# A recurrent mixer's pieces in a new order, two half-width products side by side, and a feed-forward's second weights prepared a turn later

## The reference

```python
delta = shifted - x                                   # x normalized, shifted by a token
z = tanh((x + delta * mu_x) @ W_x1.T)                 # 5 mixes x rank 32 = 160 columns
r_mu, w_mu, k_mu, v_mu, g_mu = z @ W_x2 + x_bias      # a mix factor for each
r, k = (x + delta * r_mu) @ W_r.T, (x + delta * k_mu) @ W_k.T
w = tanh((x + delta * w_mu) @ A_w.T) @ B_w.T + b_w    # decay; the inner rank is 64
v, g = (x + delta * v_mu) @ W_v.T, (x + delta * g_mu) @ W_g.T
# per head, over tokens:  o = r (S + u k v);  S = exp(-exp(w)) S + k v
o = norm_by_head(o) * gn_weight + gn_bias
out = (o * silu(g)) @ W_o.T

# feed-forward: ternary weights with one scale a row
h = x @ (tern(w_fc) * s_fc).T + gate * (x @ v.T @ fast_b.T @ u.T)
out = relu(h)**2 @ (tern(w_proj) * s_proj).T
```

## Time and profile before

| | before |
|---|---|
| time, median of 3 runs | 3333.32 us (3331.25 to 3335.09) |
| time of the profiled execution | 3332.47 us |
| its span | 3330.7 us |
| PE busy | 3141.0 us, 94% |
| DVE, ACT, POOL busy | 2521.4, 1984.0, 784.5 us |
| granted PE clock, mean | 0.958 |
| mixer | 0 to 767 us |
| first feed-forward's set-up, up to its first product | 771 to 812 us |

### The profile page before, as it was taken

The page is one execution under the profiler, slowest core; times in us unless marked ns, Lnnn a source line. Parts: engine busy times, 40 slices in busy tenths (PEclk is TensorE's granted clock), DMA queues, the critical chain, the costliest instruction groups (busy, mean ns, idle before and its releaser), DMA issues. The chain is left out here.

```text
span 3330.7 us, 78935 instructions
## 1 busy us (share of the span) xinstructions
PE 3141.0 (94%) x31780; PEld 1962.2 (59%) x31780; DVE 2521.4 (76%) x4844; ACT 1984.0 (60%) x2967; POOL 784.5 (24%) x920
## 2 busy tenths in 40 slices
PE   7999999995999589999999999999999999987999
PEld 3666666663888445555555555555555555546888
DVE  6877777755888368878878788788787887827887
ACT  2545555533666217676767676667676767775665
POOL 3444455432223201011021020110210201011222
PEclk8999999986999759999999999999999999998999
DMA  1000000003111512122222131222221312103111
GB/s 53 15 21 21 27 27 27 21 16 103 51 51 52 108 29 46 25 46 50 46 50 46 25 70 25 46 50 46 50 45 25 70 26 45 37 4 102 51 58 39
DMA packets 110301, 145.50 MB, mean 44 GB/s; under 512 B 21745, under 2 KB 94209, under 8 KB 109153
## 3 DMA queue, kind: packets, MB, share of 16 engines
q1 hardware_dynamic: 108728, 136.78, 17.6%
q0 software_dynamic: 768, 2.77, 0.4%
q10 hardware_dynamic: 440, 0.90, 0.2%
HBM read 53.79 MB, written 38.24 MB: 28 GB/s over the span
## 5 line engine op out<-in xcount | busy, mean ns | idle before, releaser
L1883 DVE TENSOR_REDUCE b_half_max<-banks 128x1 f32<-128x512 f32 x2048 | 1305.0, 685 | 300.9 <-PE banks L1556 184.4
L1807 ACT ACTIVATE b_p_t<-banks 128x1024 f32<-128x1024 f32 x1024 | 1039.6, 1026 | 372.7 <-PE banks L1556 231.6
L1632 PE MATMUL banks<-b_k_stack,b_q_stack 62*128 62x512 f32 x2048 | 836.1, 481 | 35.3 <-issue 19.4
L1694 PE MATMUL banks<-b_q_stack,b_k_stack 64*128 64x512 f32 x2048 | 832.5, 469 | 8.5 <-ACT b_p_t L1807 7.7
L1648 PE MATMUL banks<-b_p_t,b_v 128*17 128x256 f32 x8192 | 628.4, 385 | 0.2 <-ACT b_p_t L1807 0.2
L1694 PEld LDWEIGHTS banks<-b_q_stack,b_k_stack 64*128 64x128 f32 x2048 | 344.5, 185 | 372.8 <-issue 323.2
L1632 PEld LDWEIGHTS banks<-b_k_stack,b_q_stack 62*128 62x128 f32 x2048 | 342.0, 188 | 85.2 <-DVE b_half_max L1883 34.0
L1556 PE MATMUL banks<-b_unit,b_tables 64*128 64x64 bf16 x4096 | 373.3, 197 | 0.0
L1137 ACT ACTIVATE ffn_relu<-banks,ffn_scale_fc 128x512 f32<-128x512 f32 x256 | 176.1, 688 | 206.0 <-PE banks L1069 206.0
L1082 PE MATMUL banks<-ffn_proj_t,ffn_r_hi 128*128 128x256 f32 x1024 | 262.2, 289 | 2.7 <-DVE ffn_r_lo L1263 2.5
L1556 PEld LDWEIGHTS banks<-b_unit,b_tables 64*128 64x128 bf16 x4096 | 186.3, 96 | 120.9 <-issue 72.2
(11 more groups left out here) (246 smaller groups left out, 4941.1 us busy)
## 6 DMA issues: line engine op xcount, KB each, us to landing
ffn_x<-x SPq DMA_DIRECT2D x32, 512.0 KB, 3.9
b_q_stack<-b_qk_hi SPq DMA_DIRECT2D x252, 64.0 KB
b_k_stack<-b_qk_hi SPq DMA_DIRECT2D x252, 64.0 KB
a_x<-hidden_states SPq DMA_DIRECT2D x16, 512.0 KB, 4.2
x<-a_x SPq DMA_DIRECT2D x16, 512.0 KB, 2.9
x<-ffn_x SPq DMA_DIRECT2D x16, 512.0 KB, 2.8
b_x<-x SPq DMA_DIRECT2D x8, 1024.0 KB, 5.7
x<-b_x SPq DMA_DIRECT2D x8, 1024.0 KB, 4.4
```

The source lines that it names most:

```text
L1632: last = pe.matmul(m, q_stack[rows, slot, qb * P:(qb + 1) * P], k_stack[rows, slot, half * BANK:(half + 1) * BANK], start=True, stop=not h ...
L1694: last = pe.matmul(out, k_stack[stack, slot, kb * P:(kb + 1) * P], q_stack[stack, slot, half * BANK:(half + 1) * BANK], start=True, stop=n ...
L1807: act.activation(p_t[use % P_BUFS][:, :, :], scores[use % 2], ACT.Exp, scale=slopes()[pair][0]).then_inc(p_made, 1)
L1883: dve.tensor_reduce(half_max[:, (pair + rg * PAIRS) * QB + qb, half:half + 1], misc.at["max", g, turn], axis=AX.X, op=ALU.max, negate=True ...
```

## The change

It has four parts.

1. `low` is gone as a piece. `last_mix_and_low(c)` makes the last 64 rows of z for chunk c in the left half of PE's columns and the gate's low-rank product of chunk c - 1 in the right half, with the four matmuls (two of each) alternating. For this `gate_low` and `w_b` now live in partitions 64 to 127.
2. The turns' orders on all four engines are new, and the chunk's beginning (moments, normalize, turn, difference, first_mix, the first part of z) stands a turn earlier: c + 3 instead of c + 2. mix_in 0 and 2 of chunk c + 2 and pair_products 0 of chunk c + 1 stand at the end of turn c instead of the beginning of the next.
3. In the new orders of PE and ACT, output 2 stands ahead of output 1.
4. The first feed-forward prepares the projection's weights (scales, comparisons, ternary rows, transposes, row of scales) in the second chunk's `normalize`, which runs beside `up(0)`. `down(0)` waits for them.

In the diff below the hunk at 420 is PE's order in the mixer, that at 570 ACT's; those at 1005 and 1264 are the feed-forward on PE and on DVE.

```diff
+            def last_mix_and_low(c):
+
+                ranked, low = c < CHUNKS, c >= 1
+                if ranked:
+                    bz, (used, n) = ring.take(("z", c, 1), (z_made, 2 * c + 2))
+                    pe.wait_ge(used, n)
+                    pe.wait_ge(mixed_x_made, c + 1)
+                if low:
+                    bl, (used, n) = ring.take(("low", c - 1), (low_made, c))
+                    pe.wait_ge(used, n)
+                    pe.wait_ge(*mixed(c - 1, 0))
+                for kt in range(KT):
+                    if ranked:
+                        last = pe.matmul(bz[0:GATERANK, :], w_x1[:, kt, P:P + GATERANK], mixed_x[:, kt, :], start=kt == 0, stop=kt == KT - 1,
+                                         tile_position=(0, 0))
...
+                    if low:
+                        last = pe.matmul(bl[GATERANK:P, :], w_a[:, kt, :], mix(0)[:, kt, :], start=kt == 0, stop=kt == KT - 1,
+                                         tile_position=(0, GATERANK))
...
@@ -400,40 +420,39 @@
                 on(c + 1, keys)
-                on(c, carry_over, 0)
-                on(c, pair_products, 2)
-                on(c, carry_over, 1)
-                on(c, output, 0)
-                on(c + 1, queries)
-                on(c + 2, turn, 0)
+                on(c + 1, values, 0)
+                on(c, output, 2)
+                on(c + 3, turn, 0)
+                on(c + 3, turn, 1)
+                on(c, pair_products, 3)
                 on(c, output, 1)
...
                 on(c + 1, gates, 0)
                 on(c + 1, values, 1)
...
@@ -551,36 +570,36 @@
+                on(c + 3, take_turned, 0)
+                on(c, output, 2)
+                on(c + 3, take_turned, 1)
+                on(c + 1, level, 4)
+                on(c, pair_products, 3)
+                on(c + 1, take_gates, 0)
                 on(c, output, 1)
...
@@ -986,24 +1005,32 @@
+            def prepare_projection():
+                for turn, m, at, count in ternary_turns()[1]:
+                    turn_ternary(turn, HT + m, at, count, banks[:, 5 + turn % 2, :], 2)
+                for kt in range(KT):
+                    pe.wait_ge(diagonal_made, kt + 1)
+                    if kt:
+                        pe.wait_ge(row_made, 1)
+                    pe.matmul(banks[:, 7, 0:P], ones[:, :], diagonal[:, kt, :], start=True, stop=True).then_inc(row_ready, 1)
...
-                yield from steps(2)
+                yield
+                if c == 1 and first_use:
+                    prepare_projection()
+                yield
...
             def down(c):
                 par = c % 2
+                if c == 0 and first_use:
+                    pe.wait_ge(tern_t_made, FC_TURNS + PROJ_TURNS)
+                    pe.wait_ge(row_made, KT)
...
@@ -1232,7 +1264,10 @@
+                yield
+                if c == 1 and first_use:
+                    find_scales(proj, KT, HT, scale_proj, HT, 3)
+                yield
...
+                elif c == 1 and first_use:
+                    prepare_projection()
```

More of the change, by code:

```diff
@@ L732, in vector @@
             for c in TURNS:
+                on(c, level, 6)
+                on(c + 1, mix_in, 0)
+                on(c + 1, mix_in, 2)
                 on(c, pair_products, 0)
@@ L1271, in down @@
                     dve.wait_ge(y_ready, use + 1)
+                    if use == 0 and first_use:
+                        dve.wait_ge(row_made, KT)
                     if use >= 2:
```

293 lines of the change are left out of this document (139 added, 154 removed).

## The result

The changed kernel takes 3412.6 us (median of 4 runs, 3404.1 to 3418.1); the kernel before took 3334.2 (4 runs). The ratio is 1.0229, with a 95% interval of 1.0202 to 1.0256. The forecast was 3344 with a range up to 3367: the direction was right and the size far off, 78 us where 11 stood. The profiled execution spans 3415.6 us. The last instruction of the mixer on DVE starts at 845.7 us where before it stood at 766.8. So 78.9 of the 84.9 us by which the two profiled spans differ (3415.6 and 3330.7) are lost in the mixer.

The account below looks back on a forecast made before the run. PE's own work was taken to bound the kernel. Mixer +12.7 and feed-forward set-up -1.5 gave +11.2 us on the profiled 3332.47, 3343.7, and with the median 0.85 above, 3344; range 3315 to 3367.

Parts of the forecast that it names:

- the pair: Mixer, PE: gate's low-rank product beside the last mix takes 1.92 us, saving 1.80 a chunk (bounds 0 and 1.86).
- two more entries of mix_in: Mixer, PE: mix_in 4 and 6, now apart, enter that form twice more at 0.10 us: +0.2 us a turn.
- wait for a_z: Mixer, PE: the wait for the tanh of the mix factors goes: -0.43 us a turn.
- normalize's slip: Mixer, PE: turning chunk c + 3 waits for DVE's normalize: +0.35 us a turn (bounds 0 and 1).
- output 2 before output 1: Mixer, PE: values 1 waits for ACT's copy of output 1, +2.47 us a turn (bounds 0.43 and 4.24).
- the clock: Mixer, PE: turns with a lowered granted clock were carried over unchanged, so the sum had no term for it.
- The output wait: PE's stand ahead of values 1 for ACT's chain: 3.84 us of instructions, 4.24 with handoffs, 2.47 uncovered a turn.
- rival (c): Mixer, PE: standing still lets the clock fall in ten more turns for 2.7 us each: 3371 us, chance 0.15.
- The head: Mixer's start: chunk 1 reaches mixed_x ahead of DVE's first mix_in, which then stands later: +4.9 us.
- Rival (a): Mixer, PE: the new wait isn't there or is covered, and the pairs pay: 3308 us, chance 0.15.
- The feed-forward: First feed-forward's set-up: first product 10.4 us sooner, mostly lost before down(0): -1.5 us (bounds -10.4 and +2).
- Rival (b): First feed-forward's set-up: the head start is mostly kept: 3336 us, no change, chance 0.20.

Follow-up runs that it names:

- e9: e3 with the gate's low-rank product in z's column half, z's two matmuls issued first, then its two: 3359.3 us, ratio 1.0068.
- e3: Changed kernel with add_x 4 behind tree level 2 on POOL and output 1 ahead of output 2 on PE and ACT: 3342.5 us.
- e1: Changed kernel with only add_x 4 moved behind tree level 2 on POOL: 3405.2 us, ratio 1.0207.
- e7: e3 with the four matmuls of z and low not alternating, z's two issued first, then low's two: 3343.9 us, ratio 1.0031.
- e2: Changed kernel with only output 1 put ahead of output 2 again on PE and ACT: 3387.9 us, ratio 1.0155.
- e5: Kernel before with only the change's feed-forward part, its mixer left as before: 3333.4 us, ratio 0.9997.
- e16: Kernel before with two unused 1.2 us reductions on DVE ahead of normalize, no order changed: 3370.0 us, ratio 1.0104.

## Why the prediction came out as it did

One full turn, 406.15 to 455.72, against the mean of 42.83 and 43.25 before: +6.5 us. By the prediction's steps:

| step | forecast, us | measured, us | from |
|---|---|---|---|
| the pair | -1.80 | -1.7 to -1.85 | block 1.87; e9 against e3 |
| two more entries of mix_in | +0.20 | +0.20 | all ten: 5.09 in e3, 4.89 before |
| wait for a_z | -0.43 | -0.43 | gone |
| normalize's slip | +0.35 | +2.56 | transposes 437.44 to 440.88, 3.44, against 0.88 |
| output 2 before output 1 | +2.47 | +0.96, 2.15 in e1 | PE L332's wait |
| the clock | 0 | +5.1 | 441.1 to 451.4 at half clock |
| sum | +0.79 | +6.6 | |

**The pair** was right, and e9 shows it alone. What I would add is e7: the alternating order of issue isn't needed.

**The output wait** was right in place and chain (3.84 us forecast, 4.4 found). At full clock (e1) it is 2.15 us for the forecast 2.47. In the changed kernel it is smaller, 0.96, because gates 0, which covers it, runs at half clock and takes 3.73 us where the earlier trace rows has 1.77 for a product: two losses share the same time.

**The step that failed first is "With the handoff I take +0.35 us (bounds 0 and 1)".** The sum took normalize's 1.4 us from a turn in which POOL was not in its way. The new order on POOL puts add_x 4 behind root and two tree levels, beside normalize. One VectorE instruction waited it out, 2.08 us where 0.41 is usual, and two were lengthened by the levels. e1, which moves add_x alone, ends TensorE's wait for a_xn; its longest normalize instruction between 100 and 700 us is 0.95 us. What POOL runs beside the DVE work on the path was in the order and wasn't looked at, although the prediction itself took 1.6 us for slower DVE work beside POOL in the feed-forward. The Trainium skill has the rule (SBUF — State Buffer, section SBUF: two separate sides): between a GpSimd instruction and a VectorE one that is in a two-port mode, or has two inputs in SBUF while GpSimd's reads SBUF, a shared pair of ports is an exclusive lock, held for the whole instruction, and whichever comes second is fully blocked. The trace agrees with it here: the excess of 1.7 us is nearly all of the 1.9 that was left of add_x when the instruction came (438.05, add_x to 439.98). By that rule the upper bound of this step would have been about 2.0 us more, an estimate from add_x's length. One row does not fit it: POOL's power in the kernel before, in the last section. In e3 add_x, moved behind level 2, does the same to a tree level, 2.05 us where it takes 0.42:

```profile
418.54 0.43 DVE L681 TENSOR_TENSOR a_q_up<-a_q_up,a_decay 128x256 f32<-128x256 f32 x1
419.68 2.05 DVE L681 TENSOR_TENSOR a_q_up<-a_q_up,a_decay 128x256 f32<-128x256 f32 x1
```

Nothing waits for that one in time to matter.

**The step that failed worst is the clock, which the sum put at nothing**: "Such turns I carry over unchanged." It stood only in rival (c), "If the clock falls in ten more turns for 2.7 each: 3371", held at 0.15. Both of these numbers were too small: the clock fell in all full turns, for some 5 us in the one shown. Over the mixer it cost 54.7 us, over all runs 53 (195 against 142). The 2.7 came from the single fall in the earlier trace rows, which starts and ends within a turn that stands still for only 0.43 us. Its reason was the output wait, with the small matmuls ahead of it. That is not what the runs show: e2, which has no output wait, lost about as much to the clock (190) as the kernel that had both (195), and in the changed kernel most falls begin behind the wait for a_xn. And I treated it as an addition that is there or not, where e1 to e3 show it tied to the waits: both mends together gave 70 us, 34 of them rest and 35 clock. Without the clock the forecast of +11 would have met +24. The direction was right for its reason, the output wait, but that wait is only a part of the loss: taking it out alone gave 25 of the 78 us.

**The head** was sized too small as well: DVE's first mix_in starts at 31.85 us instead of 25.09, +6.8 where +4.9 was forecast.

**Rival (a)** (no wait) was rightly low, and its time was wrong too. e3 has almost no waits and takes 3342.5, not 3308: the clock takes back more (18) than the order saves (10). The undisturbed turn there is 1.0 and not 2.0 us shorter because the transposes go at the pace of normalize (1.8 us for 0.88).

**The feed-forward** was right: -1.5 forecast with bounds -10.4 and +2; e5 has -1.8 us against the runs of before, with an interval of -6.7 to +4.7. The head start (11.7 us for the forecast 10.4) and its loss behind DVE's work in the next turn are both in the trace, down(0) 1.2 us later where 1.1 sooner was forecast. In e5, behind the mixer of before, the first product comes 10.4 us sooner, as forecast, and down(0) 2.4 us later (801.75 and 829.70 against the earlier trace rows). Rival (b) is refuted.

No version beat both kernels. e3_both is the best of the new order and is not told apart from the kernel before (1.0017, 0.9996 to 1.0038).

## What to carry to other kernels

When a new order moves work on VectorE's critical path, read what GpSimd runs at that moment as well: a 2 us GpSimd instruction can be added nearly whole to a 0.4 us one. Where TensorE is busy almost all the time, give the clock a term of its own in the sum: the worst turn of before (2.7 us) for each of 13 turns would have been 35 us, still under the 53 measured, and a saving of 1 us in 43 is smaller than one such fall. Undo waits together before judging an order: each mend alone showed 7 and 25 us of 70.

## What was not expected of the hardware

- Two products in different column halves ran side by side although the program issues all passes of one and then all of the other (e7: starts 0.01 to 0.02 us apart, 1.87 us for eight passes; in one half, e9, 3.58 us).
- Not every GpSimd instruction slowed normalize. add_x over 1024 columns did (2.08 us for one), and tree levels over 256 columns did (0.62 and 0.83). But in the kernel before, the power of 16 columns spans 2.92 us beside four normalize instructions that take 1.37 in all, as long as alone. By the rule quoted above it should have blocked them, unless its span is not the time for which it holds the ports, which no run here tells:

```profile
424.05 1.37 DVE L604 TENSOR_SCALAR a_xn<-a_x,a_mean_var,a_norm_rstd 128x256 f32<-128x256 f32 x4
422.63 2.92 POOL L825 TENSOR_TENSOR a_rstd<-a_rstd,a_half 128x16 f32<-128x16 f32 x1
```
- TensorE busy without a gap does not keep its clock: a turn of e3, 47.66 us busy of 47.66, had a granted clock of 0.86, and the fall at 442.7 came after 25 us without a pause; another turn with the same pieces had 1.00 and took 41.86 us. And TensorE idle for 1.84 us a turn kept it in seven turns of ten (e16).
